# Denominators on TensorE, residual sums two steps late, list products on GpSimd, and a last tile in two halves

## What is computed

```
def step(carry, kv_t):          # per batch and channel, over 256 times
    y_t = (e1 * aa + e2 * vt) / (e1 * bb + e2)
    ...
x = x + tanh(g_xattn) * wkv(decay, first, layernorm(x), ctx)
logits = flat @ Wg + bg         # flat = layernorm(x), 2048 tokens; 4 experts, top 2
for i in range(4):              # each expert takes the 512 tokens of highest probability
    sel_p, sel_idx = top_k(where(assigned, probs[:, i], -inf), 512)
    h = gelu(flat[sel_idx] @ W1[i])          # 512 -> 2048
    out = out.at[sel_idx].add(h @ W2[i] * p) # 2048 -> 512
x = x + tanh(g_ffn) * out
```

## Time and profile before

| | us |
|---|---|
| median of 3 runs | 473.99 |
| lowest, highest | 473.29, 474.87 |
| profiled execution, its time | 473.74 |
| profiled execution, its span | 471.8 |
| mean granted TensorE clock | 0.958 |
| PE, DVE, ACT, POOL busy | 409.2, 291.8, 313.4, 109.7 |

### The profile page before, as it was taken

One profiled execution on the slowest core, in us unless ns is written; L12 is line 12 of the kernel. 1 busy time (PEld: TensorE's weight loads), 2 busy tenths in 40 slices (PEclk: granted clock), 3 DMA queues, 4 the chain that ended last, 5 costly groups with the idle time before them and its releaser, 6 DMA issues.

```text
span 471.8 us, 6973 instructions
## 1 busy us (share of the span) xinstructions
PE 409.2 (87%) x1991; PEld 196.2 (42%) x1991; DVE 291.8 (62%) x596; ACT 313.4 (66%) x487; POOL 109.7 (23%) x126
## 2 busy tenths in 40 slices
PE   2686877812699999999999999999999999999991
PEld 1342443501464444444444444444444444444440
DVE  7999999988589986474575174457516435550000
ACT  6698888998569874766778790577879157760000
POOL 0787846601300002521000412100041210001111
PEclk9999999965599999999999999999999999999997
DMA  7985110399500629399000959500095510001211
GB/s 257 353 328 208 44 69 23 125 343 355 179 1 1 272 95 365 99 152 356 1 0 14 380 131 265 192 0 1 6 366 150 79 22 0 0 0 18 29 22 22
DMA packets 36182, 62.79 MB, mean 133 GB/s; under 512 B 14336, under 2 KB 14464, under 8 KB 34112
## 3 DMA queue, kind: packets, MB, share of 16 engines
q1 hardware_dynamic: 32064, 53.32, 32.6%
q0 software_dynamic: 3664, 8.65, 9.0%
q10 hardware_dynamic: 432, 0.54, 0.3%
HBM read 46.78 MB, written 12.58 MB: 126 GB/s over the span
## 4 chain that ended last, share of the span: by engine, by line
PE 74%; DVE 16%; issue 3%; ACT 2%; DMA 2%; POOL 2%; DVEq 0%; POOLq 0%
PE ps L813 35%; PE ps L798 26%; PE ps L778 7%; DVE arena L1278 6%; PE ps L741 2%; DVE arena L1297 2%; DVE arena L1308 2%; DMA arena<-xn_table,idx 1%; DVE arena L1533 1%; PE ps L617 1%; ACT early L874 1%; DMA small<-in_scalars 1%; POOL arena L1134 1%; PE ps L733 1%; DVE arena L1655 0%
## 5 line engine op out<-in xcount | busy, mean ns | idle before, releaser
L813 PE MATMUL ps<-arena 128*128 128x512 f16 x768 | 166.8, 379 | 0.0
L798 PE MATMUL ps<-arena,early 128*128 128x512 f16 x576 | 124.8, 379 | 0.0
L813 PEld LDWEIGHTS ps<-arena 128*128 128x128 f16 x768 | 74.6, 98 | 89.2
L798 PEld LDWEIGHTS ps<-arena,early 128*128 x576 | 56.4, 98 | 67.9
L1041 ACT ACTIVATE arena<-ps,up 128x512 f32<-128x512 f32 x64 | 43.8, 684 | 59.8 <-PE ps L798 41.2
L1707 DVE SCALAR_TENSOR_TENSOR arena<-arena,h_down 128x512 f32 x48 | 36.0, 751 | 58.8 <-ACT arena L1044 58.8
L1213 POOL DMA_INDIRECT result<-arena,idx x16 | 29.2, 1826 | 185.9 <-DVE arena L1735 122.7
L1044 ACT ACTIVATE arena<-arena,h_down 128x512 f32 x64 | 46.2, 721 | 8.7 <-ACT arena L1041 0.2
L1735 DVE TENSOR_SCALAR arena<-ps,yscale 128x512 f32<-128x512 f32 x16 | 12.0, 748 | 60.5 <-PE ps L813 49.2
L1686 DVE SCALAR_TENSOR_TENSOR early<-w_raw,down,early 128x2048 f16<-128x2048 f32 x16 | 37.0, 2345 | 18.8 <-ACT early L998 18.8
L1047 ACT ACTIVATE arena<-rows,down x64 | 45.2, 706 | 0.0
(11 more groups left out here) (224 smaller groups left out, 449.6 us busy)
## 6 DMA issues: line engine op xcount, KB each, us to landing
w_raw<-in_L_ffn_W SPq DMA_DIRECT2D x4, 4096.0 KB, 14.3
rows<-in_L_ffn_W SPq DMA_DIRECT2D x3, 4096.0 KB, 17.6
rows<-in_L_ffn_W SPq DMA_DIRECT2D x4, 1024.0 KB, 9.6
result<-rows SPq DMA_DIRECT2D x3, 1024.0 KB, 6.8
early<-in_ctx SPq DMA_DIRECT2D x2, 1024.0 KB, 6.9
rows<-in_x SPq DMA_DIRECT2D x2, 1024.0 KB, 12.0
xn_table<-arena SPq DMA_DIRECT2D x4, 512.0 KB, 5.1
xn_table<-arena SPq DMA_DIRECT2D x2, 1024.0 KB, 4.6
```

Source lines behind the costliest of these rows:

```text
L798: last = nc.tensor.matmul(ps[:, PH[q], :], w[:, k, at], t[:, k, :], start=n == 0, stop=n == 3 * CT - 1)
L813: last = nc.tensor.matmul(ps[:, PY[s % 2], :], h[:, t, s * P:(s + 1) * P], w[:, t, :], start=t == 0 and n == 0, stop=t == HT - 1 and n == 2)
```

## The change

It is made of nine parts.

1. Long units have no `den` on VectorE. TensorE adds state times exp(-first) onto the transposed keys in PSUM by a matmul with a diagonal matrix (`add_first`, a 128x128 f32 matrix by 512 columns), and ScalarE's logarithm reads PSUM. The four diagonals are made by ScalarE once, before unit 0.
2. In long units `residual` and its `xt` and `router` come two steps late, none in the second step of a group and two in the first; TensorE transposes the keys of unit u + 2 at the end of step u.
3. At step 2 `xt(2)` stands ahead of the products of unit 4.
4. In the threshold rounds 0 to 2 the next candidate comes from the count of reached candidates in one instruction; the sums behind it (`add_steps`, `base`, `nxt`) come after `spot`.
5. GpSimd makes three small matrices (`less16`, `group16`, `tri16`), `in_a` in four instructions and `put` of expert 0.
6. SP issues the last quarter of the second weights only when the third gathered tile has landed.
7. A second `keep_warm` stands behind `others_round(1)`.
8. The last block of the last down product is computed, scaled and added to the result as two halves of 256 columns.
9. Some semaphores are joined.

```diff
+def residuals_of(step):
+    k = step % CT
+    if step <= CT or step > CT * (NG - 1):
+        return (), ((step - 1,) if step > 0 else ())
+    return ((step - 2,) if k == 0 else ()), ((step - 1,) if k == 0 else () if k == 1 else (step - 2,))
@@ sync
+            sp.wait_ge(c_tok[SPT], 16)
             first_w2(3, (4,))
@@ tensor
+            def keys(u):
                 if u >= 2:
-                    pe.wait_ge(s_den if GROUPS[g] > 1 else s_num, u - 1)
+                    pe.wait_ge(s_num, u - 1)
+                    if long(u - 2):
+                        pe.wait_ge(s_ln, u - 1)
...
+            def add_first(u):
+                size = length(u)
...
+                pe.wait_ge(s_fix, u + 1)
+                nc.tensor.matmul(pair(u, size, 2 * size), first_diag[:, u % CT, :], state[:, u % 2, size:2 * size],
+                                 start=False, stop=True, skip_group_check=True).then_inc(s_denp, 1)
...
             for u in range(UNITS):
+                early, late = residuals_of(u)
+                if u == 0:
+                    xt(0)
+                for r in early:
+                    xt(r + 1)
+                if long(u):
+                    add_first(u)
+                elif u + 2 < UNITS:
+                    keys(u + 2)
+                if u == LATE_M:
+                    xt(u)
                 if u + 2 < UNITS:
-                    kv(u + 2)
+                    products(u + 2)
...
-                xt(u)
-                if u > 0:
-                    router(u - 1)
+                for r in late:
+                    if u != LATE_M:
+                        xt(r + 1)
+                for r in early + late:
+                    router(r)
+                if long(u):
+                    keys(u + 2)
...
                 others_round(1)
+                keep_warm(WARM)
                 pe.wait_ge(b_taken, 2)
...
+            def last_halves():
+                for n in range(2):
+                    cols = slice(n * D // 2, (n + 1) * D // 2)
...
@@ scalar
+                if long(u):
+                    act.wait_ge(s_denp, u - shorts(u) + 1)
+                    there = pair(u, length(u), 2 * length(u))
@@ gpsimd, behind the gather of zeros
+            pool.wait_ge(b_hot, 1)
+            for a in range(ST):
+                nc.gpsimd.tensor_scalar(in_a[:, 0, :, a], slot_a[:, 0, :], float(a), None, ALU.is_equal).then_inc(s_lists, 1)
+            pool.wait_ge(s_lists, 3 + ST)
+            nc.gpsimd.tensor_tensor(put[:, 0, :, :]..., in_a[:, 0]..., vals[:, 0]..., ALU.mult).then_inc(s_lists, 1)
             gather(0)
@@ vector, sums(u)
-                nc.vector.scalar_tensor_tensor(den[:, n, 0:size], ...).then_inc(s_den, 1)
+                if not long(u):
+                    nc.vector.scalar_tensor_tensor(den[:, n, 0:size], ...).then_inc(s_den, 1)
@@ vector, threshold rounds
-                nc.vector.tensor_scalar(digit[:, 0:1], steps_up[:, 0:1], -1.0, float(1 << shift0(r)), ALU.add, ALU.mult)
-                nc.vector.tensor_tensor(cand[:, 0:1], digit[:, 0:1], nxt[:, 0:1], ALU.bitwise_or)
+                if r < EXACT0:
+                    nc.vector.tensor_scalar(cand[:, 0:1], took[:, r:r + 1], float(1 << shift0(r)), plus,
+                                            ALU.mult, ALU.add).then_inc(b_cand, 1)
```

More of the change, by code:

```diff
@@ L76, in shift0, with ones0 @@
     return DIGIT0 * (ROUNDS0 - 1 - r)
+def ones0(r):
+    return sum(1 << shift0(i) for i in range(r + 1))
 def tiles_of(g):
@@ L141, in program @@
     out_rows = out.rearrange("b s d -> (b s) d")
+    out_halves = out.rearrange("b s (a d) -> (b s a) d", a=2)
     out_v = out_rows.rearrange("(t p) d -> p t d", p=P)
@@ L275, in program @@
         cnt = sb("cnt", [P, 2])
+        took = sb("took", [P, ROUNDS0])
+        sum_next = sb("sum_next", [P, EXACT0])
+        sum_base = sb("sum_base", [P, EXACT0])
         spot = sb("spot", [P, LANES0], F16)
@@ L478, in length, with long, shorts @@
             return GROUPS[u // CT] * SEQ
+        def long(u):
+            return GROUPS[u // CT] > 1
+        def shorts(u):
+            return sum(not long(i) for i in range(u + 1))
         def starts(ap, u):
@@ L578, in kv, with products @@
                         pe.wait_ge(s_ek, t + 1)
-                    nc.tensor.transpose(pair(u, length(u) + i * P, length(u) + (i + 1) * P), ek[:, t % RING, ct * P:(ct + 1) * P], ident)
+                    last = nc.tensor.matmul(pair(u, length(u) + i * P, length(u) + (i + 1) * P), ek[:, t % RING, ct * P:(ct + 1) * P], ident,
+                                     start=i == 0 or not long(u), stop=True, is_transpose=True,
+                                            skip_group_check=True)
+                last.then_inc(s_keys, 1)
+            def add_first(u):
+                size = length(u)
+                if u == CT:
+                    pe.wait_ge(setup_a, 5 + CT)
+                pe.wait_ge(s_fix, u + 1)
+                nc.tensor.matmul(pair(u, size, 2 * size), first_diag[:, u % CT, :], state[:, u % 2, size:2 * size],
+                                 start=False, stop=True, skip_group_check=True).then_inc(s_denp, 1)
+            def products(u):
+                g, ct = u // CT, u % CT
                 if u >= 2:
@@ L817, in down_block @@
                 last.then_inc(c_y, 1)
+            def last_halves():
+                for n in range(2):
+                    cols = slice(n * D // 2, (n + 1) * D // 2)
+                    pe.wait_ge(c_yout, START + (E - 1) * ST + (ST - 2))
+                    for t in range(HT):
+                        for i, (h, w) in enumerate(((h_hi, w2_hi), (h_hi, w2_lo), (h_lo, w2_hi))):
+                            last = nc.tensor.matmul(ps[:, LAST[n], 0:D // 2], h[:, t, (ST - 1) * P:ST * P], w[:, t, cols],
+                                                    start=t == 0 and i == 0, stop=t == HT - 1 and i == 2)
+                    last.then_inc(c_y, 1)
             def next_expert(e):
@@ L837, in _ @@
             up_product(E - 1)
-            for s in range(ST):
+            for s in range(ST - 1):
                 down_block(E - 1, s)
+            last_halves()
         @block.scalar
@@ L890, in _ @@
                 set_decay(k, 0)
+            act.wait_ge(s_id, 16)
+            for k in range(CT):
+                nc.scalar.activation(first_diag[:, k, :], ident, ACT.Copy, scale=chan[:, 3, k:k + 1]).then_inc(setup_a, 1)
             start(act, c_tokhi, c_w1hi, c_w2hi, c_gelu, c_hhi, c_w2sum, c_w1sum)
@@ L1107, in scales1 @@
                     hold(pool, "pool")
-                    nc.gpsimd.tensor_scalar(var1[:, some], sq1[:, there], 1.0 / D, EPS, ALU.mult, ALU.add).then_inc(s_var1, 1)
+                    nc.gpsimd.tensor_scalar(var1[:, some], sq1[:, there], 1.0 / D, EPS, ALU.mult, ALU.add).then_inc(s_nb, 1)
                 else:
@@ L1249, in _ @@
                 added(e)
-            scatter(E - 1, range(ST))
-            added(E - 1)
+            scatter(E - 1, range(ST - 1))
+            pool.wait_ge(c_yscs, START + 2 * E + 2)
+            for n in range(2):
+                cols = slice(n * D // 2, (n + 1) * D // 2)
+                pool.wait_ge(c_yout, START + (E - 1) * ST + ST + n)
+                hold(pool, "pool")
+                nc.gpsimd.indirect_dma_start(out_halves, bass.IndirectOffsetOnAxis(ap=idx_half[:, n:n + 1], axis=0),
+                                             y_c[:, (ST - 1) % 2, cols], None,
+                                             bounds_check=2 * N - 1, compute_op=ALU.add).then_inc(c_last[n], 16)
+            pool.wait_ge(c_add[0], E * 16 * ST // 2)
+            pool.wait_ge(c_add[1], (E * ST // 2 - 1) * 16)
+            pool.wait_ge(c_last[0], 16)
+            pool.wait_ge(c_last[1], 16)
         @block.vector
@@ L1357, in _ @@
                 scan(u)
+                for r in residuals_of(u)[0]:
+                    residual(r)
                 for t in STATS.get(u, ()):
@@ L1363, in _ @@
                 sums(u)
-                if u > 0:
-                    residual(u - 1)
+                for r in residuals_of(u)[1]:
+                    residual(r)
                 if u == 0:
```

190 lines of the change are left out of this document (120 added, 70 removed).

## The result

The changed kernel takes 470.01 us (median of 6 executions, 468.55 to 470.95) against 474.07 for the kernel before: a ratio of 0.9915, interval 0.9890 to 0.9941. It is faster, by 4.1 us; I had said 7. The six executions lie in two groups, three at 468.55 to 469.12 and three at 470.9 to 470.95; the last two experiments are about that. The profiled one took 469.02 with a span of 467.0, so it is of the lower group, and against the span before (471.8) it gained 4.8 us.

The account below looks back on a forecast made before the run. VectorE bounds the long units; TensorE is busy throughout from 139 to 462 us, untouched. 473.74 less 5.0 (recurrence), 0.4 (step 2), 0.6 (list to weights) and 0.7 (end) is 467.04; forecast 467.1, range 463.9 to 470.5.

Parts of the forecast that it names:

- VectorE is the bound, ScalarE 7 us behind: Long units before the change: VectorE busy 53.38 of 54.14 us sets the pace, ScalarE stands 7.16 us behind it.
- the add at 1.02 us: TensorE's new matmul in long units: takes as long as the logits, 1.02 us, between 0.86 and twice 1.02.
- step 2: Recurrence: the transposes of x, moved ahead of the products, spare VectorE's residual a wait; 0.4 us gained, 0 to 0.43.
- The recurrence, 5.0 us: Long units: denominators off VectorE gain 6.0 us at most, less 1.0 for waits: 5.0, between 3.0 and 6.0.
- The prediction's own sign against itself: Recurrence: the prediction is wrong if ScalarE still waits several us for TensorE.
- The late residuals are what leaves room: Long units: y and x asked for one step later, about 3.8 us, which takes in ScalarE's backlog of 1 to 2.
- My allowance of 1.0 us for waits: Long units: 1.0 us taken off the 6.0 us gain for waits on ScalarE's backlog.
- Rival 3: Recurrence: TensorE, at 3.80 of 3.83 us, passes any wait on; step 4.2 instead of 4.08, 468.6 to 469.6; chance 0.18.
- Threshold, 1.2 to 2.1 us on VectorE: Threshold rounds and list: fewer instructions, indicators and products off VectorE; 1.2 to 2.1 us gained there, hidden behind GpSimd.
- The list, 0.65 lost: List of expert 0: waits for GpSimd's indicators and product behind its gather of zeros; at 118.35 instead of 117.70 us.
- Gather and clock: List to first products: holding the last quarter gains 1.2 us, full clock from the second `keep_warm` 1.0 us.
- The end, 0.7 us: Last block in halves: scaling gains 0.28 us, the last addition's landing 0.4; 0.7 together, 0 to 1.8.

Follow-up runs that it names:

- the last two experiments: Four unused transposes ahead of TensorE's waits for GpSimd's rows: on the changed kernel 468.58 us, on the kernel with GpSimd's better order 464.26 us.
- GpSimd's better order: GpSimd's small scales reordered, on the changed kernel with residuals one step late and expert 0's indicators and product back on VectorE (466.06 us): 463.99 us.
- thin add: The changed kernel with the matmul of `add_first` over 8 columns instead of 512: 470.47 us.

## Why the prediction was off

The time lies 2.9 us above the forecast, inside the range and near its upper end. By the spans the sum was 6.7 us gained, and 4.8 came.

**VectorE is the bound, ScalarE 7 us behind:** right, as the earlier trace rows say. VectorE's gain (7.9 forecast, 8.0), the add at 1.02 us (L628 in any step) and step 2 (0.4 forecast, 0.32) came as worked out.

**The recurrence, 5.0 us:** this step failed; to the last logits 2.33 us came, 0.32 of it step 2's, so 2.0. Of the 3.0 missing, 1.3 are missing in the long units (3.66 came) and 1.7 in what follows them. The prediction's own sign against itself, ScalarE still waiting several us for TensorE, did show: 3.4 us in four waits for `add_first`. Two terms were mis-sized. First, "The late residuals are what leaves room" is the wrong way round: with one step VectorE waits 2.2 us more for quotients and the whole is still faster, since two steps put double work at the group's first step; that cost 1.0 us at scan 17, and 2.5 us in the median (1.6 against the lower group). My allowance of 1.0 us for waits was for ScalarE's backlog. The waits that came are at another place, 5.7 us of TensorE for GpSimd's rows at steps 6, 10 and 14, which the prediction did not name, although GpSimd's small scales stand ahead of its rows in the code. Second, I carried the gain of the long units over unshortened. At their end (step 16 to 17) 2.90 us became 4.44, 1.5 us lost. Residuals 14 and 15 both stand in that step, and GpSimd's quotient of 15 is late because `add_first` stood behind TensorE's wait for the rows. With one-step residuals the step still takes 4.39 us, with a wait of 1.41 for that quotient, so the lateness of part 2 is not what makes it long; GpSimd's better order brings it to 3.44.

**Rival 3, TensorE's order couples the engines,** came nearest in time (468.6 to 469.6 against a profiled 469.02; the median lies 0.4 above it) and in mechanism, but not for its reason: the thin add shows that at full clock the 3.80 us of 3.83 are worth 0.7 us in seven steps, not the bound. In-order waiting at the seams is.

**Threshold, 1.2 to 2.1 us on VectorE:** from the last logits to the one-hot rows 20.74 us became 19.13, 1.61 gained. **The list, 0.65 lost:** from the last logits to `idx` 23.56 became 24.06, 0.50 lost. (The prediction's own terms, 117.2 and 0.9, make 118.1 and thus 0.4 lost; its 118.35 is 0.25 too high.) Right by the sum, and yet the reading behind it, that VectorE's gain is hidden whole in any case, was wrong: it is hidden only because part 5 puts GpSimd's gather of zeros ahead of the products. Without part 5 the list comes 1.56 us earlier.

**Gather and clock:** from the list to the first products 8.81 became 7.69 us, 1.1 gained (1.2 forecast); the 16 products 0.9 (1.0). TensorE's clock was full from 124 us on (0.68 from 122 to 124), before from 129 (0.90 from 128 to 130); the second `keep_warm` was not tried apart. TensorE waits at `w2_top` as said, but little: its weight loads stand 0.41 us, its matmuls 0.13. From the last logits to the gapless stretch 1.19 us were gained, 0.6 forecast, within its ends. What the hold has to do with it is not what I said: taking it out alone changed nothing in the executions without a spell; with a late list the first gather lands after 3.5 to 3.7 us either way.

**The end, 0.7 us:** 9.88 became 8.47, less 0.13 for two half products: 1.3. The scaling gave 0.27 as said; the transfer lands after 3.8 instead of 4.9 us, where I took 0.4. This term was too small: half the bytes took 1.1 us off the landing.

**The two groups.** Half of the executions carry another 1.9 us, which no term foresaw. A spell of half clock at 40 us costs 1.6. In three profiles it starts 0.4 to 1.1 us behind TensorE's waits at step 6, in two more (denominators back, thin add) within a wait of TensorE near it. It stands in neither of the two profiles with filler, and none of the changed kernel's four executions with filler has the upper group's time. That the upper group is this spell is thus likely, but no profile of an execution of that group was had, so it isn't shown. Nor is it shown what decides, in one and the same program, whether a spell comes.

## What to carry to other kernels

When the bound engine is relieved, read the in-order streams of the others at the seams of the loop, where the pattern breaks: there a small instruction ahead of a needed one costs more than a step's balance tells. Making results wait longer "for room" piles work up somewhere; test the plain order first. And before work is given to an idle engine, look at what stands ahead of it in that engine's order and whether the consumer waited for it before.

## What the runs showed of the chip

- TensorE's granted clock can fall to half for about 3 us in the middle of a busy stretch, behind waits of 0.7 and 0.9 us, in one execution and not in another whose instructions up to there are the same; the price is 1.6 us. Filling part of the waits with unused transposes costs nothing that the marks show; that it prevents the fall is not shown.
- Four GpSimd instructions on 16 columns take 0.95 us by themselves and 2.77 us beside two VectorE instructions with two inputs in SBUF (2.36 us together): the first two last 1.24 and 1.17 us, until the VectorE instruction beside them has ended.
- An indirect addition of half the columns lands after 3.8 instead of 4.9 us.
